# A decoder layer in float32: attention scores from 32-row tiles, a 9-column values product, residuals added on TensorE, and a new order of all engines

## The chip, the core and the metric

The kernel runs on one core of one Trainium2 chip. The metric is the device time of one execution in microseconds (us). Everything is float32.

## The reference, cut to what matters

The input `x` is 32 sequences (b) of 128 rows (s) by 128 features (d); `ctx` has the same shape. Three residual steps, each followed by a layer norm without gain:

```
# 1. self-attention, 16 heads of 8 features, keys and values through a rank-32 bottleneck
latent = (x@W_k + x@W_v) @ W_down_kv
k, v   = latent @ W_up_k, latent @ W_up_v ;  q = x @ W_q
scores = einsum('bhqd,bhkd->bhqk', q, k) / sqrt(128) * exp(-0.01*|i-j|)
x = layernorm(x + (softmax(scores) @ v) @ W_o)
# 2. second attention, over features: 8x8 weights in each head, from x and ctx
A = softmax_e(einsum('bhsd,bhse->bhde', x, ctx) / sqrt(128))
x = layernorm(x + ((ctx@Wv.T + bv) with A) @ Wo.T + bo)
# 3. experts: a norm with gain and offset, a router, the best 2 of 8 experts for each row
xf = layernorm(x, ln_g, ln_b) ;  logits = xf @ router ;  top 2, gates by softmax
each expert: layernorm(xf)*eg+eb -> clip/silu gated pair of 128x512 -> 512x128
x = layernorm(x + sum of the two gated experts)
```

## The kernel before, in words

The program has four blocks, one after the other, each with one instruction stream for every engine and semaphores between them.

The first block does attention, second attention and routing in one software pipeline. A loop runs over steps b = -1 to 38; in step b each engine does its part of several batches of different age: `on(b, lag)` is true when batch b - lag exists. Batch b has its input transposed and its queries and keys made in step b - 1, scores in step b, softmax and values product up to step b + 1, output projection and first norm in b + 2, the second attention in b + 3, its norm in b + 4, the router's norm in b + 5, router and choice in b + 6, and rank and scatter in b + 7. The order of an engine's instructions in a step is written out by hand.

Scores (`p_score`, L431): the keys of all heads stand in `kbd`, a block-diagonal image of 128 rows by 16 x 128 columns, so that one matmul of 512 columns gives four heads with the queries `qT` (128 rows) as weights. The image is made through DRAM: SP stores `kT` into a zeroed `key_image` (L250) and reads it back with four DMAs (L255). Two PSUM banks (`ps_s`) take the scores in turn. VectorE multiplies them by the decay into `sc` (L638, four a batch) and takes the row maximum of half the heads (L644, two a batch). GpSimd subtracts it (L332, `shift`, two a batch), and ScalarE exponentiates 1024 columns at a time (L551). TensorE transposes the 16 weight matrices (L411), ScalarE copies them out of PSUM (`a_pT`), and 16 matmuls sum into `acc` (`p_mix`, L422), each with one head of `vbd` as moving operand: 144 columns, 128 for the head's values in its own place with zeros around them and 16 for the row sums.

The first residual is an add on VectorE (L747) before statistics (L754), aggregation (L759), a power on GpSimd (L325, L327) and the norm `x1` (L764). After the second attention (masked gram matrix L701, maximum L725, exponential L600, `gA` L751, product L507, output L527) VectorE adds the residual (L655) and the bias (L668), takes statistics and norms into `xall` (L728). The router's norm is a statistics pair and norm again (L685, L711, L733), a gain and an offset on GpSimd (L373, L375) and a third norm `xhat` (L737). The router's choice ends in `both` on GpSimd (L379), two rank matmuls (L524, L525) and two indirect DMAs from GpSimd (L355) that put the rows into `expert_in`.

Before the loop SP issues, in this order: eleven loads of weights, the first input, all of `x` and of `ctx` (`xall`, `call`, four DMAs each of 512 KB, L224), three router parameters, the zeroing of the key images (L233). In the loop it loads each batch's `xin` and `cin` once more for the transposes (L240, L243). GpSimd issues the loads of the experts' parameters ahead of the loop (L313 to L320).

The second block works out the table of tiles from the counts (L788 on), the third runs the experts over 39 tiles of 256 rows, and the fourth gathers, adds, norms and stores.

Of the kernel before, what the change touches and what calls it, by code (L numbers as in the profile page):

```python
# [24 lines left out]
I32 = mybir.dt.int32  # L25
U32 = mybir.dt.uint32
# [10 lines left out]
def decoder_layer(nc, x, ctx_in, W_q, W_k, W_v, W_o, W_down, W_upk, W_upv, xWv, xbv, xWo, xbo,  # L37
# [9 lines left out]
    VW = D + H  # L47
# [7 lines left out]
    LOAD = 8  # L55
# [7 lines left out]

    GH = 32 // HD
    KIMG_H = HD * GH * S + S
    KIMG = GH * KIMG_H * (P // 32)
    kimg = nc.dram_tensor("key_image", [2, KIMG], F32)

    with ExitStack() as es:
# [6 lines left out]

        xall = sb("xall", [P, B, D])
        call = sb("call", [P, B, D])
        xf = sb("xf", [P, 2, D])
        gain_row = sb("gain_row", [P, D])  # L80
        offset_row = sb("offset_row", [P, D])
        rpad = sb("rpad", [P, P])
        xfT = sb("xfT", [P, S])
        top = sb("top", [P, B, E])
        thr = sb("thr", [P, MAXT]); tile_no = sb("tile_no", [P, TILES])
        idx = sb("idx", [P, 2, E], U32)
        iota_e = sb("iota_e", [P, E])
        oh = sb("oh", [P, 2, 2, E])
        both = sb("both", [P, E])
        cum = sb("cum", [P, E])  # L90
        rnk = sb("rnk", [P, 2, E])
        row_f = sb("row_f", [P, 2, 2])
        pos = sb("pos", [P, B, 2], U32)
        xhat = sb("xhat", [P, B, RW])
        fill = sb("fill", [P, 2, RW])
        earlier = sb("earlier", [P, P])
        ones = sb("ones", [P, P])
        iota_i = sb("iota_i", [P, B + 2 + 2 * E + MAXT + TILES], I32)
        st3 = sb("st3", [P, 6])
        st4 = sb("st4", [P, 6])  # L100
        mv34 = sb("mv34", [P, 2, 2]); rs34 = sb("rs34", [P, 2])
        xn = sb("xn", [P, D])
        params = sb("params", [P, E, PRM])
        bo_rows = sb("bo_rows", [P, E, D])
        ident = sb("ident", [P, P])
# [11 lines left out]
        eps_col = sb("eps_col", [P, 4])  # L117
        setup = sb("setup", [P, 8, D])
        xin = sb("xin", [P, 2, D])
        cin = sb("cin", [P, 2, D])  # L120
        x1 = sb("x1", [P, 2, D])
        xT = sb("xT", [P, 2, S])
        qT = sb("qT", [P, 2, S])
        kT = sb("kT", [P, 2, S])
        kbd = sb("kbd", [P, 2, H, S])
        vbd = sb("vbd", [P, 2, H, VW])
# [3 lines left out]
        rsum = sb("rsum", [P, 2, H])  # L130
        att = sb("att", [P, D])
        attT = sb("attT", [P, D])
        res1 = sb("res1", [P, D])
        st1 = sb("st1", [P, 6])
        mv1 = sb("mv1", [P, 2])
        rs1 = sb("rs1", [P, 1])
# [8 lines left out]
        res2 = sb("res2", [P, D])  # L145
        st2 = sb("st2", [P, 6])
        mv2 = sb("mv2", [P, 2])
        rs2 = sb("rs2", [P, 1])


        zrow = sb("zrow", [P, 4 * D])
        mv3, mv4 = mv34[:, 0, :], mv34[:, 1, :]
        rs3, rs4 = rs34[:, 0:1], rs34[:, 1:2]
# [4 lines left out]
        acc = ps_a[:, 0:VW]  # L158
        m0a, m0b = ps_m[:, 0, 0, :], ps_m[:, 0, 1, :]
        m1a, m1b = ps_m[:, 1, 0, :], ps_m[:, 1, 1, :]  # L160
        m2a, m2b = ps_m[:, 2, 0, :], ps_m[:, 2, 1, :]
        m0c, m2c, m2d = ps_m[:, 0, 2, :], ps_m[:, 2, 2, :], ps_m[:, 2, 3, 0:E]


        ld_w = sem("ld_w"); ld_x = sem("ld_x"); ld_c = sem("ld_c"); zeroed = sem("zeroed")
        x_in = [sem("x_in0"), sem("x_in1")]; c_in = [sem("c_in0"), sem("c_in1")]
        cst = sem("cst"); su_v = sem("su_v"); su_p = sem("su_p"); su_a = sem("su_a")
        x_trans = sem("x_trans"); xT_ready = sem("xT_ready")
        qk_done = sem("qk_done"); q_ready = sem("q_ready"); k_ready = sem("k_ready")
        v_done = sem("v_done"); v_ready = sem("v_ready")  # L170
        k_clear = sem("k_clear"); k_stored = [sem("k_stored0"), sem("k_stored1")]
        k_spread = [sem("k_spread0"), sem("k_spread1")]
        scored = sem("scored"); decayed = sem("decayed"); maxed = sem("maxed")
        shifted = sem("shifted"); exped = sem("exped")
        p_trans = sem("p_trans"); pT_ready = sem("pT_ready"); mixed = sem("mixed")
        sums_inv = sem("sums_inv"); att_ready = sem("att_ready"); att_trans = sem("att_trans")
        attT_ready = sem("attT_ready"); projected = sem("projected"); res1_ready = sem("res1_ready")
        stat1 = sem("stat1"); mean1 = sem("mean1"); rstd1 = sem("rstd1"); x1_ready = sem("x1_ready")
# [4 lines left out]
        res2a = sem("res2a"); res2_ready = sem("res2_ready"); stat2 = sem("stat2"); mean2 = sem("mean2"); rstd2 = sem("rstd2")  # L183
        x2_ready = sem("x2_ready")
        stat3 = sem("stat3"); mean3 = sem("mean3"); xn_ready = sem("xn_ready")
        gained = sem("gained"); xf_ready = sem("xf_ready")
        stat4 = sem("stat4"); mean4 = sem("mean4"); xhat_ready = sem("xhat_ready"); rstd34 = sem("rstd34")
        top_ready = sem("top_ready"); oh_ready = sem("oh_ready"); both_ready = sem("both_ready"); ranked = sem("ranked")
        cum_ready = sem("cum_ready"); rank_read = sem("rank_read"); row_ready = sem("row_ready"); pos_ready = sem("pos_ready")
        tagged = sem("tagged"); filled = sem("filled"); scattered = sem("scattered")  # L190
        f_trans = sem("f_trans"); fT_ready = sem("fT_ready"); routed = sem("routed"); logits_ready = sem("logits_ready")
        ld_p = sem("ld_p"); ld_e = sem("ld_e"); zero_row = sem("zero_row"); rcst = sem("rcst")
# [926 lines left out]
```

## Time and profile before

| | us |
|---|---|
| median of 3 runs | 889.16 (888.18 to 890.44) |
| profiled execution, its own time | 885.5 |
| its span, first to last instruction | 883.8 |
| mean granted TensorE clock, share of 2.4 GHz | 0.924 |

Of the span, the first block takes about the first 539 us, the table of tiles until 548, the experts until about 826 and the last block the rest. In the profile, "PE" is TensorE's matmuls and "PEld" its weight loads, DVE is VectorE, ACT ScalarE, POOL GpSimd, SP SyncE; an engine name with a q is its queue. A float32 matmul shows as two instructions. The end of a matmul is modelled; the starts are what can be compared.

### The profile page before, as it was taken

What the parts mean: (1) busy time and instruction counts of PE and PEld (TensorE: products, weight loads), DVE (VectorE), ACT (ScalarE), POOL (GpSimd) and SP (SyncE); (2) the same over time, 40 slices, a digit from 0 to 9 for tenths busy, and PEclk for the clock granted to TensorE, in tenths of its full rate; (3) what the DMA queues carried; (4) which work ended last, traced back from release to release, by engine and by line L of the source; (5) the groups of instructions that cost most, each with busy time, mean ns of one, the idle gap of its engine ahead of it and who ended that gap; (6) DMA issues with size and microseconds to landing.
All of it is one profiled execution on the core that took longest, in us unless ns stands there. A gap on an engine that the chain in (4) does not pass through costs nothing. (4 is left out here: it accounts for less than half of the span.)

```text
span 883.8 us, 14582 instructions
## 1 busy us (share of the span) xinstructions
PE 646.6 (73%) x3961; PEld 534.8 (61%) x3961; DVE 588.7 (67%) x1819; ACT 322.4 (36%) x756; POOL 458.8 (52%) x785
## 2 busy tenths in 40 slices
PE   1189988888889898989898530888888888885000
PEld 1057877777767676767677420777787878874000
DVE  2056886868687777778787433577777777774487
ACT  1034544444444443444444200444444444442000
POOL 9034547676666666666667671044343443434244
PEclk9999999999999999999999755899999999998555
DMA  8711111111111111111110000455555555551243
GB/s 196 146 43 40 43 43 31 52 35 48 37 45 38 45 37 46 46 37 55 28 49 16 16 24 20 152 167 165 151 171 159 171 163 157 176 167 52 79 120 92
DMA packets 86912, 74.18 MB, mean 84 GB/s; under 512 B 10896, under 2 KB 69840, under 8 KB 86832
## 3 DMA queue, kind: packets, MB, share of 16 engines
q1 hardware_dynamic: 76832, 60.14, 24.0%
q0 software_dynamic: 5392, 11.01, 4.0%
q10 hardware_dynamic: 4608, 2.10, 0.8%
q8 instruction: 33, 0.54, 0.3%
q14 instruction: 47, 0.39, 0.2%
HBM read 58.04 MB, written 15.17 MB: 83 GB/s over the span
## 5 line engine op out<-in xcount | busy, mean ns | idle before, releaser
L422 PE MATMUL ps_a<-vbd,pT 128*128 128x144 f32 x1024 | 149.8, 290 | 1.2 <-ACT pT L535 0.5
L422 PEld LDWEIGHTS ps_a<-vbd,pT 128*128 128x128 f32 x1024 | 134.8, 190 | 20.8 <-issue 15.5
L332 POOL TENSOR_TENSOR sc<-sc,rowmax 128x1024 f32<-128x1024 f32 x64 | 121.5, 1898 | 41.9 <-DVE rowmax L644 41.9
L431 PE MATMUL ps_s<-kbd,qT 128*128 128x512 f32 x256 | 132.6, 601 | 5.4 <-DMA kbd<-key_image 5.4
L638 DVE TENSOR_TENSOR sc<-ps_s,decay 128x512 f32<-128x512 f32 x128 | 87.4, 683 | 57.1 <-PE ps_s L431 56.4
L962 ACT ACTIVATE x2c<-ps_m,prt 128x256 f32<-128x256 f32 x117 | 55.5, 474 | 139.0 <-PE ps_m L927 139.0
L913 POOL DMA_INDIRECT expert_out<-yt,dest x78 | 82.8, 1062 | 34.3 <-issue 30.2
L938 PEld LDWEIGHTS ps_t<-wot,hid 128*128 128x128 f32 x624 | 92.6, 191 | 11.3 <-DVE hid L998 2.5
L535 ACT ACTIVATE pT<-ps_t 128x512 f32<-128x512 f32 x128 | 72.7, 596 | 70.0 <-PE ps_t L411 67.3
L925 PE MATMUL ps_m<-xg,w2t 128*128 128x256 f32 x234 | 74.0, 398 | 32.2 <-DVE hid L994 29.4
L938 PE MATMUL ps_t<-wot,hid 128*128 128x128 f32 x624 | 94.7, 275 | 1.9 <-DVE hid L998 1.9
L551 ACT ACTIVATE sc<-sc 128x1024 f32<-128x1024 f32 x64 | 68.0, 1062 | 48.4 <-POOL sc L332 48.4
L644 DVE TENSOR_REDUCE rowmax<-sc 128x8 f32<-128x1024 f32 x64 | 77.8, 1215 | 0.1
L355 POOL DMA_INDIRECT expert_in<-xhat,pos x64 | 65.0, 1016 | 19.6 <-POOL pos L348 9.9
L905 POOL COPY bot<-bo_rows 128x128 f32 x39 | 12.1, 310 | 114.6 <-DVE yt L1004 114.6
L411 PE MATMUL ps_t<-ident,sc 128*128 128x128 f32 x512 | 71.3, 273 | 0.0
L927 PE MATMUL ps_m<-xg,w1t 128*128 128x256 f32 x234 | 70.5, 383 | 0.0
L325 POOL TENSOR_TENSOR rs<-mv,eps_col 128x1 f32<-128x1 f32 x64 | 12.1, 189 | 111.6 <-DVE mv L759 80.1
L411 PEld LDWEIGHTS ps_t<-ident,sc 128*128 128x128 f32 x512 | 60.0, 141 | 16.3 <-issue 16.3
L994 DVE SCALAR_TENSOR_TENSOR hid<-ps_m,prt,sil 128x256 f32<-128x256 f32 x117 | 53.0, 481 | 23.9 <-ACT sil L968 23.8
L649 DVE RECIPROCAL rsum<-ps_a 128x16 f32<-128x16 f32 x32 | 8.2, 258 | 81.3 <-PE ps_a L422 81.3
L925 PEld LDWEIGHTS ps_m<-xg,w2t 128*128 128x128 f32 x234 | 36.0, 194 | 39.1 <-issue 32.6
(194 smaller groups left out, 1305.8 us busy)
## 6 DMA issues: line engine op xcount, KB each, us to landing
w2t<-in_L_ffn_W_dram SPq DMA_DIRECT2D x39, 256.0 KB, 2.7
w1t<-in_L_ffn_W_dram SPq DMA_DIRECT2D x39, 256.0 KB, 2.9
wot<-in_L_ffn_Wo_dram SPq DMA_DIRECT2D x39, 256.0 KB, 3.6
kbd<-key_image SPq DMA_DIRECT2D x128, 64.0 KB, 1.9
xst<-expert_in SPq DMA_DIRECT2D x39, 130.0 KB, 2.0
g<-expert_out SPq DMA_DIRECT2D x32, 128.0 KB, 2.1
xin<-in_x_dram SPq DMA_DIRECT2D x32, 64.0 KB, 2.0
xall<-in_x_dram SPq DMA_DIRECT2D x4, 512.0 KB, 6.7
```

Source lines behind the costliest of these rows:

```text
L332: pool.tensor_tensor(sc[:, slot], sc[:, slot], rowmax[:, slot, :].unsqueeze(2).to_broadcast([P, HALF, S]), ALU.subtract).then_inc(shifted, 1)
L411: mm = pe.transpose(ps_t[:, quarter % 2, j * S:(j + 1) * S], sc[:, 2 * par + quarter // 2, 4 * (quarter % 2) + j, :], ident[:, :])
L422: mm = pe.matmul(acc, pT[:, quarter, j * S:(j + 1) * S], vbd[:, par, h, :], start=(h == 0), stop=(h == H - 1))
L431: pe.matmul(ps_s[:, quarter % 2, :, :], qT[:, par, :], kbd[:, par, 4 * quarter:4 * quarter + 4, :], start=True, stop=True).then_inc(scored, 1)
L535: return act.activation(out, in_, ACT.Copy)
L551: act.activation(sc[:, slot], sc[:, slot], ACT.Exp).then_inc(exped, 1)
L638: dve.tensor_tensor(sc[:, slot, j:j + 4, :], ps_s[:, quarter % 2, :, :], decay[:, :].unsqueeze(1).to_broadcast([P, 4, S]), ALU.mult).then_ ...
L644: dve.tensor_reduce(rowmax[:, slot, :], sc[:, slot], AX.X, ALU.max).then_inc(maxed, 1)
L913: pool.indirect_dma_start(ys_dram[:, :], bass.IndirectOffsetOnAxis(ap=dest[:, n, a:a + 1], axis=0), yt[:, par, a, :], None).then_inc(y_out ...
L925: pe.matmul(ps_x2[c], w2t[:, par, P * c:P * c + P], xg[:, par, :], start=True, stop=True)
L927: pe.matmul(ps_x1[c], w1t[:, par, P * c:P * c + P], xg[:, par, :], start=True, stop=True).then_inc(up, 1)
L938: mm = pe.matmul(ps_y[par][:, a * P:(a + 1) * P], hid[:, par, c, a * P:(a + 1) * P], wot[:, par, c, :], start=(c == 0 and a == 0), stop=(c ...
```

## The change

All of it is in the first block.

- Scores: the key image has 128 rows by 4 x 128 columns (`kbd[P, 3, GH, S]`): rows 32g to 32g+31 hold heads 4g to 4g+3. One matmul has 32 rows of `qT` as weights and 32 rows of `kbd` as moving operand, again 512 columns and four heads. Two such matmuls, on neighbouring 32-row strips and into the two banks of `ps_s`, are issued behind each other with one semaphore. The image is stored and read back by one DMA each, without zeroing in SBUF, and `xT`, `qT`, `kT` and `kbd` have three buffers.
- Values product: `v9` holds 9 columns a head (8 values and a one for the sum); each matmul writes its own 9 columns of `acc`. ScalarE writes `v9`.
- Residuals: `ident` x `xall` is accumulated onto the projection, and `first` x `bo_row` and `ident` x `x1` onto the second output; statistics and norms read PSUM.
- The router's norm is worked out from the second norm's variance v: (v(1 + eps) + eps^2)^-0.5 scales `centred`, the centred rows times the gain; its own statistics are gone.
- Softmax: heads 0 to 7 are exponentiated by eight ScalarE instructions of 128 columns with the negated maximum as bias; heads 8 to 15 as before with GpSimd's shift.
- Loads: `x` and `ctx` come four batches at a time, from SP, every fourth step; the transposes read `xall` and `call`; the zeroing of the images is issued by ScalarE; the experts' parameters are loaded behind GpSimd's work of step 0.
- Each engine's loop runs over steps s = -2 to 39 with a new order, and the waits are rewritten for it.

```diff
 # SyncE
-                for dst, src, done in ((xall, x, ld_x), (call, ctx_in, ld_c)):
-                    for i in range(0, B, LOAD):
-                        sp.dma_start(dst[:, i:i + LOAD, :], ...)
+                sp.dma_start(xall[:, 1:4, :], x[1:4].rearrange("b s d -> s b d")).then_inc(ld_x, 16)
+                sp.dma_start(call[:, 0:4, :], ctx_in[0:4].rearrange("b s d -> s b d")).then_inc(ld_c, 16)
...
+                for b in range(B):
+                    spread_keys(b)      # wait k_ready; store kT; wait k_stored, scored of b - 3; read into kbd
+                    if b % 4 == 0 and b + 4 < B:
+                        n = b + 4
+                        sp.dma_start(xall[:, n:n + 4, :], x[n:n + 4].rearrange("b s d -> s b d")).then_inc(ld_x, 16)
+                        sp.dma_start(call[:, n:n + 4, :], ctx_in[n:n + 4].rearrange("b s d -> s b d")).then_inc(ld_c, 16)
 # GpSimd
+                for s in range(first_step, last_step + 1):
+                    if ever(s - 7): tag(s - 7)
+                    if ever(s - 4): rstd4_of(s - 4)
+                    if ever(s - 6): count(s - 6)
+                    if ever(s - 3): rstd2_of(s - 3)
+                    if ever(s - 3): router_rows(s - 3)
+                    if ever(s - 7): place(s - 7)
+                    if ever(s - 7): scatter(s - 7)
+                    if ever(s + 1): shift(s + 1)
+                    if ever(s - 5): choices(s - 5)
+                    if ever(s - 1): rstd1_of(s - 1)
+                    if s == 0:
+                        # params (10 DMAs) and bo_rows
 # TensorE
-                def p_score(b, quarter, par):
-                    ...
-                    pe.matmul(ps_s[:, quarter % 2, :, :], qT[:, par, :], kbd[:, par, 4 * quarter:4 * quarter + 4, :],
-                              start=True, stop=True).then_inc(scored, 1)
+                def score(b, pair):
+                    if pair == 0:
+                        pe.wait_ge(q_ready, b + 1)
+                        pe.wait_ge(k_spread[b % 2], 16 * (b // 2 + 1))
+                        before(pe, decayq[2], b)
+                        before(pe, decayq[3], b)
+                    else:
+                        pe.wait_ge(decayq[0], b + 1)
+                        pe.wait_ge(decayq[1], b + 1)
+                    for i in range(2):
+                        rows = slice(32 * (2 * pair + i), 32 * (2 * pair + i) + 32)
+                        mm = pe.matmul(ps_s[:, i, :, :], qT[rows, b % 3, :], kbd[rows, b % 3, :, :], start=True, stop=True)
+                    mm.then_inc(scored, 1)
-                        mm = pe.matmul(acc, pT[:, quarter, j * S:(j + 1) * S], vbd[:, par, h, :],
-                                       start=(h == 0), stop=(h == H - 1))
+                        mm = pe.matmul(acc[:, h, :], pT[:, i, j * S:(j + 1) * S], v9[:, b % 2, h, :], start=True, stop=True)
+                    pe.matmul(m0a, attT[:, :], wo[:, :], start=True, stop=False)
+                    pe.matmul(m0a, ident[:, :], xall[:, b, :], start=False, stop=True).then_inc(projected, 1)
...
+                    pe.matmul(m2a, oT[:, :], xwoT[:, :], start=True, stop=False)
+                    pe.matmul(m2a, first[:, :], bo_row[:, :], start=False, stop=False)
+                    pe.matmul(m2a, ident[:, :], x1[:, b % 2, :], start=False, stop=True).then_inc(x_out, 1)
+                def trans_f(s):
+                    b = s - 6
+                    upto(pe, x1_ready, s - 3)
+                    pe.wait_ge(xf_ready, b + 1)
+                    pe.transpose(m0c, xf[:, b % 2, :], ident[:, :]).then_inc(f_trans, 1)
...
+                for s in range(first_step, last_step + 1):
+                    if ever(s - 1): trans_p(s - 1, 1)
+                    if ever(s - 6): trans_f(s)
+                    if ever(s - 3): trans_c(s)
+                    if ever(s + 2): trans_x(s)
+                    if ever(s): score(s, 1)
+                    if ever(s + 2): queries(s)
+                    if ever(s + 2): keys(s)
+                    if ever(s - 1): trans_p(s - 1, 2)
+                    if ever(s - 3): vp(s)
+                    if ever(s - 2): trans_att(s)
+                    if ever(s - 1): trans_p(s - 1, 3)
+                    if ever(s - 3): gram_of(s)
+                    if ever(s - 6): logits(s)
+                    if ever(s - 1): mix(s - 1, 1)
+                    if ever(s - 1): mix(s - 1, 0)
+                    if ever(s - 2): project(s)
+                    if ever(s - 1): mix(s - 1, 3)
+                    if ever(s + 1): score(s + 1, 0)
+                    if ever(s): values(s)
+                    if ever(s - 3): second_out(s)
+                    if ever(s - 1): mix(s - 1, 2)
+                    if ever(s): trans_p(s, 0)
+                    if ever(s - 3): second_sum(s)
+                    if ever(s - 6): ranks(s)
 # ScalarE
+                def exp_heads(b):
+                    slot = 2 * (b % 2)
+                    act.wait_ge(maxed0, b + 1)
+                    for h in range(HALF):
+                        done = act.activation(sc[:, slot, h, :], sc[:, slot, h, :], ACT.Exp, bias=rowmax[:, slot, h:h + 1])
+                    done.then_inc(exped0, 1)
...
+                    # copy_p(s-2,3), gram_exp(s-4), exp_heads(s-1), copy_o(s-4), exp_half(s-1), copy_v(s-1),
+                    # copy_p(s-1,0), copy_x(s+2), copy_c(s-3), copy_f(s-6), copy_p(s-1,1), copy_k(s+2),
+                    # copy_q(s+2), copy_att(s-2), copy_vp(s-3), copy_p(s-1,2)
 # VectorE
+                def centred(b):
+                    dve.scalar_tensor_tensor(out=xc[:, b % 2, :], in0=m2a, scalar=mv2[:, 0:1], in1=gain_row[:, :],
+                                             op0=ALU.subtract, op1=ALU.mult).then_inc(xc_ready, 1)
...
+                for s in range(first_step, last_step + 1):
+                    # gram_max(s-3), best_index(s-6), row_max(s,1), gram_inv(s-3), second_weights(s-3) [gA],
+                    # one_hot(s-6), norm4(s-5) [xhat], stats1(s-2), aggr1(s-2), decayed_scores(s+1,1), stats4(s-4),
+                    # decayed_scores(s+1,0), norm1(s-2) [x1], aggr4(s-4), sums(s-1), heads(s-1), stats2(s-3),
+                    # aggr2(s-3), row_max(s+1,0), centred(s-3), norm2(s-3) [xall], decayed_scores(s+1,3),
+                    # own_rank(s-6), row_of(s-7), decayed_scores(s+1,2), masked_gram(s-2), best(s-5)
```

`upto(engine, semaphore, b)` waits until batch min(b, 31) has signalled. The calls of ScalarE's and VectorE's orders, and GpSimd's parameter loads, are written here as comments that list them.

## Rows read from the trace of the kernel before

**Rows 1.** Busy time by window: length, busy us and instructions per engine, clock, DMA.

```profile
300.00:400.00 100.00, 87.85 (x568) 70.36 (x567) 75.94 (x235) 44.01 (x112) 66.95 (x111) 1.00 0.15 42
500.00:520.00 20.00, 9.27 (x32) 7.11 (x32) 8.52 (x50) 2.14 (x8) 14.13 (x33) 0.50 0.06 20
580.00:700.00 120.00, 105.64 (x631) 94.56 (x632) 86.73 (x242) 54.28 (x111) 48.85 (x74) 1.00 0.53 163
```

**Rows 2.** Timeline, TensorE, the input transpose that opens a step: start, us.

```profile
96.83 0.27 PE L440 MATMUL ps_m<-ident,xin 128*128 128x128 f32 x1
108.52 0.27 PE L440 MATMUL ps_m<-ident,xin 128*128 128x128 f32 x1
...
310.39 0.27 PE L440 MATMUL ps_m<-ident,xin 128*128 128x128 f32 x1
324.81 0.27 PE L440 MATMUL ps_m<-ident,xin 128*128 128x128 f32 x1
```

**Rows 3.** Waits of TensorE, 200 to 400 us: us in total, times, longest.

```profile
PE ps_m L524 <- POOL both L379: 16.6, 14, 1.2
PE ps_m L507 <- DVE gA L751: 7.7, 14, 0.6
```

**Rows 4.** Timeline, TensorE, 300 to 315 us.

```profile
301.51 1.02 PE L431 MATMUL ps_s<-kbd,qT 128*128 128x512 f32 x2
302.36 1.14 PE L422 MATMUL ps_a<-vbd,pT 128*128 128x144 f32 x8
303.34 0.39 PE L496 MATMUL ps_m<-wo,attT 128*128 128x128 f32 x2
303.56 1.02 PE L431 MATMUL ps_s<-kbd,qT 128*128 128x512 f32 x2
...
308.67 0.36 PE L524 MATMUL ps_m<-both,earlier 128*128 128x8 f32 x2 [1.18 <-POOL both L379]
308.88 0.37 PE L525 MATMUL ps_m<-cum,ones 128*128 128x8 f32 x2
309.10 0.47 PE L527 MATMUL ps_m<-xwoT,oT 128*128 128x128 f32 x2
...
313.55 1.04 PE L411 MATMUL ps_t<-ident,sc 128*128 128x128 f32 x8
314.42 0.27 PE L482 MATMUL ps_m<-ident,att 128*128 128x128 f32 x1
```

**Rows 5.** Timeline, GpSimd and VectorE, 316 us.

```profile
316.40 1.90 POOL L332 TENSOR_TENSOR sc<-sc,rowmax 128x1024 f32<-128x1024 f32 x1
316.43 1.95 DVE L728 TENSOR_SCALAR xall<-res,mv,rs 128x128 f32<-128x128 f32 x1
```

**Rows 6.** Timeline, ScalarE, 201 us: an exponential with a bias and its successor.

```profile
201.18 0.40 ACT L600 ACTIVATE gex<-gm,gmax 128x128 f32<-128x128 f32 x1 [0.85 <-DVE gmax L725]
201.49 0.19 ACT L600 ACTIVATION_READ_ACCUMULATOR gex<-gm,gmax 128x1 f32 x1
```

**Rows 7.** Timeline, the start of the kernel, all engines.

```profile
11.29 14.87 SPq L224 DMA_DIRECT2D call<-in_ctx_dram  x4
11.63 0.79 PE L401 MATMUL ps_m<-setup 32*128 32x128 f32 x2 [0.36 <-ACT setup L535]
15.52 0.80 PE L453 MATMUL ps_m<-xT,wq 128*128 128x128 f32 x2 [1.65 <-ACT xT L535]
16.96 0.27 ACT L535 ACTIVATE kT<-ps_m 128x128 f32<-128x128 f32 x1
36.79 0.63 SPq L250 DMA_DIRECT2D key_image<-kT  x1
42.16 2.07 PE L431 MATMUL ps_s<-kbd,qT 128*128 128x512 f32 x2 [3.31 <-DMA kbd<-key_image]
```

**Rows 8.** Timeline, the last steps of the loop and the next block's first matmul.

```profile
500.78 0.57 PE L524 MATMUL ps_m<-both,earlier 128*128 128x8 f32 x2 [1.93 <-POOL both L379]
501.20 0.57 PE L525 MATMUL ps_m<-cum,ones 128*128 128x8 f32 x2
...
539.18 0.57 PE L788 MATMUL ps_a<-cum,ones 128*128 128x8 f32 x2 [11.76 <-PEq L209]
```

More of the change, by code:

```diff
@@ L201, in before, with ever, upto @@
                 eng.wait_ge(s, v)
-        def steps(step):
-            for b in range(-1, B + 7):
-                step(b, b % 2)
-        wsrc = [W_q, W_k, W_v, W_o, xWv, xWo]
+        def ever(b):
+            return 0 <= b < B
+        def upto(eng, s, b):
+            before(eng, s, min(b, B - 1) + 1)
+        first_step, last_step = -2, B + 7
         with nc.Block() as block:
@@ L530, in _, with trans_c @@
-                steps(step)
+                def trans_f(s):
[3 more added lines that the diff above has]
+                    pe.transpose(m0c, xf[:, b % 2, :], ident[:, :]).then_inc(f_trans, 1)
+                def trans_c(s):
+                    b = s - 3
+                    upto(pe, x1_ready, s - 3)
+                    pe.wait_ge(ld_c, 16 * (b // 4 + 1))
+                    pe.transpose(m0b, call[:, b, :], ident[:, :]).then_inc(c_trans, 1)
@@ new lines, in trans_x, with vp @@
+                def trans_x(s):
+                    b = s + 2
+                    upto(pe, x1_ready, s - 3)
+                    pe.wait_ge(ld_x, 16 * (1 if b == 0 else b // 4 + 2))
+                    pe.transpose(m0a, xall[:, b, :], ident[:, :]).then_inc(x_trans, 1)
+                def vp(s):
+                    b = s - 3
+                    upto(pe, xT_ready, s + 2)
+                    upto(pe, fT_ready, s - 6)
+                    pe.wait_ge(cT_ready, b + 1)
+                    pe.matmul(m0b, xwvT[:, :], cT[:, :], start=True, stop=True).then_inc(vp_done, 1)
@@ new lines, in trans_p @@
+                def trans_p(b, i):
+                    if i < 2:
+                        pe.wait_ge(exped0, b + 1)
+                        before(pe, pT_ready[i + 2], b)
+                    else:
+                        pe.wait_ge(exped1, b + 1)
+                        pe.wait_ge(pT_ready[i - 2], b + 1)
+                    for j in range(4):
+                        mm = pe.transpose(ps_t[:, i % 2, j * S:(j + 1) * S], sc[:, 2 * (b % 2) + i // 2, 4 * (i % 2) + j, :],
+                                          ident[:, :])
+                    mm.then_inc(p_trans[i], 1)
@@ L535, in copy @@
                     return act.activation(out, in_, ACT.Copy)
+                act.wait_ge(zeroed, 1)
+                for i in range(2):
+                    act.dma_start(kimg[i].rearrange("(p n) -> p n", p=P), zrow[:, :]).then_inc(k_clear, 16)
                 act.wait_ge(su_p, 1)
```

953 lines of the change are left out of this document (457 added, 496 removed).

## The prediction

> **What bounds the kernel now.** I read the windows first. From 60 to 480 us the kernel runs the attention and routing loop; from 580 to 800 it runs the expert stage, which this change does not touch. In the attention window TensorE is busy 88 of 100 us, VectorE 76, GpSimd 67, ScalarE 44 [rows 1]. Busy TensorE time is modelled, so I went to the timeline for the spacing of starts. One loop step, from one transpose of the inputs to the next, is 14.42 us (310.39 to 324.81); before the routing work joined, a step was 11.69 [rows 2]. So 26 of the 32 steps with scores (b = 6 to 31) cost 14.42.
>
> How much of a step does TensorE need? Its instructions follow each other at these pitches [rows 4]: a float32 matmul is two instructions; 512 columns cost 0.85 us the pair (301.51 to 302.36); eight instructions of 144 columns 0.98 (0.122 each); a 128-column float32 matmul 0.22; eight transposes 0.87 (0.109 each). The rows to look at are those with 8 columns: L524, L525 and L527 start 0.21 and 0.22 apart, so a two-instruction matmul costs 0.107 each whether it streams 8 or 128 columns. What is left then is the weight load. The step needs 4 x 0.85 = 3.4 for scores, 32 x 0.122 = 3.9 for the values product, 20 transposes 2.2, and 11 small matmuls 2.4: 11.9 us. The other 2.5 are stalls, of which 1.7 have a name: the rank matmul waits 1.2 us for GpSimd's `both`, the second attention 0.55 for VectorE's `gA` [rows 3]. Behind `gA` stands a stall of VectorE: the norm at L728 takes 1.95 us, from 0.03 after GpSimd's shift L332 starts to its end [rows 5]. TensorE is the bound, with 2.5 of its 14.4 us lost to the order of the engines' work.
>
> **The change part by part**, per step at the same pitches.
>
> Values product, 144 to 9 columns: the count stays 32 instructions and 32 weight loads. They fall from 0.122 to the floor of 0.107 [rows 4], 32 x 0.015 = 0.5 saved, giving 3.4. The columns fall sixteenfold and the time by an eighth. Less than nothing is excluded, since the 8-column rows show the floor directly; 0.5 is nearly certain.
>
> Scores from 32-row tiles in pairs: still 4 matmuls of 512 columns. Fewer rows alone buy nothing: L401 with 32 rows takes 0.79 where L453 with 128 rows takes 0.80, both at the low clock [rows 7]. A gain needs the two tiles of a pair to run beside each other. No row shows that. Bounds: each pair takes 0.85 (full overlap), or 1.71 (none). Each matmul is two instructions on the same rows that must follow each other, so the first tile's second half can lie beside the second tile's first half, and three half-matmuls remain: 3 x 0.427 = 1.28. I take that, in between. Against it stands the change of tile shape, twice per pair, four times a step. A 128-column transpose is recorded at 0.27 us and its neighbour starts 0.11 after [rows 2, 4], so 0.16 of it is still in the pipe; if the engine had to empty and then load weights uncovered (0.107), a change costs 0.16 + 0.1 = 0.26, four of them 1.0. Below that it can cost nothing. I take half, 0.5. Scores: 2 x 1.28 + 0.5 = 3.1, bounds 1.7 and 4.4, against 3.4 now.
>
> The skill bears on this place: the Trainium skill, TensorEngine Tiling, Key Properties, says that a change of tiling mode drains the engine while tiles of one mode run in parallel. By that rule the four changes cost their full 1.0 and the scores 3.6, so they would gain nothing; no row here shows a change of mode in a full stream.
>
> Residuals on TensorE: `ident` x `xall`, `first` x `bo_row`, `ident` x `x1` are three more small matmuls at 0.22: +0.66. The new step sum: values 3.4, transposes 2.2, small ones 2.4 + 0.66, scores 3.1 = 11.8 (8.7 without scores), against 11.9. The work of TensorE hardly falls; what can fall is the stall.
>
> VectorE, now 10.9 a step (76 per 100 us, [rows 1, 2]). Removed: two residual adds, the bias add, the third statistics pair, the norm `xn`, the copy into the diagonal (to ScalarE), some 1.2 together at 0.15 to 0.25 each; `norm2` now reads PSUM. Added: `centred`, 0.2. The stall behind the shift does not go: `norm4` is of the same form as L728, and it and `gA` now stand right behind `row_max(s,1)`, which releases the one shift that stays. So about 1.9 us is paid again in that place [rows 5]. Sum about 10. GpSimd: one of two shifts of 1.9 goes, the norm's `pow` chain gains one instruction: from 9.6 to about 8.5. ScalarE, 6.3 now: eight exponentials of 128 columns with a bias instead of one of 1024. The `gex` row of that shape starts its successor 0.31 later [rows 6]: 8 x 0.31 = 2.5 for about 1.1, with the value copy 0.2: 7.9. All stay below TensorE.
>
> The loops, followed through a step (TensorE time from its start). `score(s+1,0)` ends near 8.6; VectorE's two decays, `stats4` and `norm1` take 2.1; TensorE has 3.3 of other work before `trans_f` needs `x1_ready`: 1.2 slack. `gA`: the row maximum at 6.8, the shift until 8.9 at worst, `second_out` due near 9: no slack. `exped0` at about 8.5, due at 10.1 for `trans_p(s,0)`. `both` moves to a place two microseconds ahead of `ranks`. So the old 1.2 stall has cover, and the old 0.55 may stay. I put 0.35 of stalls: period 11.8 + 0.35 = 12.15. 26 steps x (14.42 - 12.15) = 59 us.
>
> The key path: SP stores and spreads in two DMAs for five, and no longer issues `xin` and `cin` each step; three buffers let it run a step ahead. It took 5.4 us from the store's issue to the first score (36.79 to 42.16, [rows 7]) against a period of 12: hidden. The 512 KB that SP issues every fourth step stand behind the spread and ahead of the next store, hidden by the same slack.
>
> The head: keys of batch 0 are ready at 17 (16.96, [rows 7]) and stored only at 36.79, because SP is held 15 us issuing the bulk loads of `call`, and rows and clears behind it. Those loads now come four batches at a time and the clear goes by ScalarE's queue at the start. First score at 17 + 5.4 = 22.4 for 42.2. The GpSimd fill of 1 MB may lie beside it: 20 saved, bounds 10 and 22. The ten parameter loads that GpSimd issues now stand behind its second shift; its next work is a step later. Early steps: two near 9.5 and four near 11.3 make 64 behind `score(0,0)`, against the 66 from 42.2 to 108.5 [rows 2, 7], and the first pair is at the low clock: nothing counted.
>
> The tail (steps 32 to 38, before L788 at 539.2, [rows 8]) is latency, with PE waiting for VectorE and GpSimd; the router rows no longer need a second `pow` round: 5 saved, bounds 0 and 12.
>
> **Sum.** 59 + 20 + 5 = 84 off the profiled execution's 885.5 (span 883.8 and 1.7 around it): 801.5. The median of the runs, 889.2, lies 3.7 above that execution, so 805 on its scale.
>
> **The rivals.**
> 1. Forecast: partial overlap, a step of 11.7 to 12.6. With 26 steps that is 793 to 817; with head and tail, 785 to 825. Chance 0.48.
> 2. Full overlap and free changes: scores 1.7, period 10.4 + 0.3 = 10.7, 38 us more: 767. For it: the tiles lie on separate rows and in separate PSUM banks. Against it: the two halves of one matmul, and loops with little slack. Chance 0.13.
> 3. The tiles bring nothing: pairs at 1.71 and full changes, 8.7 + 4.4 = 13.1, with stalls 13.45: 34 us more, 839. For it: no row shows overlap. Chance 0.2. The rule above would give 8.7 + 3.6 + 0.35 = 12.65, or 818, within rival 1.
> 4. A new wait: `gA` held by the shift makes `second_out` late by a microsecond, and copies, `second_sum` and the next statistics slide with it: 13.2 a step, 832. For it: the lock of [rows 5] now lies just ahead of `gA`. Against it: a slower TensorE gives slack back. Chance 0.12.
> 5. Slower: the clock. In the thin tail the granted clock is 0.50 with TensorE busy 9 of 20 us [rows 1], and L524 to L525 is 0.42 for 0.21 [rows 4, 8]. The new loop streams few columns through most of a step. If the chip takes that for idleness, weight loads double and a step is some 23. The gain of 84 is gone when the low clock holds for about 84 / (32 x 11.5) = 23% of the loop; at half of it, 985. Against it: the transposes and small matmuls now fill such stretches at clock 1.00 and it never fell there. Chance 0.06. The Trainium skill, TensorE: Matmul & The Clock Gate, Part 4, says transposes do not count as busy time for the clock; by it this rival would be likelier than I put it, and the steady clock of 1.00 with eight transposes in a row neither bears it out nor refutes it.
> 6. No change to speak of: 0.01.
>
> **How the numbers follow.** The range takes rivals 1, 3, 4 and, down to the edge, 2: 768 to 850 (839 plus a head that saves 10 less). Below lies half of rival 2, above rival 5 and a piece of 3, some 0.17. Of this kernel 0.3% is about what a measurement can tell. Faster 0.93, same 0.01, slower 0.06.
>
> **What would show it.** Right: the L422 counterpart at 0.107 pitch with 9 columns; starts of the input transposes 12.1 apart; a first score near 22; granted clock 1.00 to the tail; `norm4` or `gA` at 1.9 us. The pair's four starts tell the tiles: second tile starting with the first tile's second half means 1.28, at once with the first means 0.85, after it 1.71; a gap ahead of each pair is the change of shape. Wrong: a granted clock of 0.5 inside the loop, or a period above 13 with TensorE waiting for `gA`, `x1_ready` or ScalarE's copies.

## The result, and the profile after

The changed kernel takes 974.95 us (969.61 to 978.86, 4 runs) against 888.95 (888.18 to 890.44, 4 runs) of the kernel before: a ratio of 1.096, with a 95% interval of 1.089 to 1.103. It is 86 us slower where 84 us less had been forecast. Here and below a time is the median of all runs of a kernel, a ratio that of its fast runs alone, which leaves out the slowest run of e2, e8, e9 and e11. The profiled execution took 971.45 us, its span is 969.6, and its mean granted clock is 0.739.

The page of the changed kernel: busy time by engine, then the clock row of the picture in 40 slices.

```profile
span 969.6 us, 16064 instructions
...
PE 798.2 (82%) x4153; PEld 671.6 (69%) x4153; DVE 578.3 (60%) x1596; ACT 371.6 (38%) x1012; POOL 404.8 (42%) x785
...
PEclk9998755766656575565656665569999999999555
```

Read the last line first. In the loop most of the clock digits are 5 to 7, in tenths of full speed, where [rows 1] had 1.00. The windows of the changed kernel, in the columns of [rows 1]:

```profile
300.00:400.00 100.00, 100.00 (x523) 83.98 (x522) 63.56 (x166) 47.17 (x144) 48.81 (x96) 0.64 0.15 39
780.00:880.00 100.00, 88.10 (x526) 78.42 (x524) 72.20 (x202) 45.40 (x93) 40.71 (x62) 1.00 0.54 164
```

TensorE is now busy all of the time, no wait of TensorE is left in this window, and its clock is 0.64. Of the two levels, 1.2 and 2.4 GHz, it holds the lower for (1 - 0.64) / 0.5 = 72% of the time. VectorE and GpSimd are busy for less of it than in [rows 1]. The expert stage, second row, is as fast as before. Within one stretch of the loop the two levels lie beside each other:

```profile
300.00:306.00 6.00, 6.00 (x30) 5.73 (x29) 2.82 (x8) 1.99 (x4) 1.56 (x6) 0.50 0.00 0
306.00:313.00 7.00, 7.00 (x54) 5.91 (x55) 5.85 (x15) 5.87 (x20) 5.11 (x7) 0.99 0.11 31
313.00:326.00 13.00, 13.00 (x54) 10.16 (x51) 7.22 (x21) 3.64 (x11) 5.62 (x15) 0.50 0.07 22
```

Seven microseconds at full clock hold as many instructions (54) as the next thirteen at half. Which stretch comes before the fall is read in the timeline of TensorE:

```profile
306.06 1.13 PE L525 MATMUL ps_s<-kbd,qT 32*128 32x512 f32 x4
307.12 0.49 PE L454 MATMUL ps_m<-xT,wq 128*128 128x128 f32 x2
...
309.24 1.93 PE L546 MATMUL ps_a<-v,pT 128*128 128x9 f32 x16
311.03 0.47 PE L445 MATMUL ps_m<-wo,attT 128*128 128x128 f32 x2
311.33 0.39 PE L446 MATMUL ps_m<-xall,ident 128*128 128x128 f32 x2
311.56 0.96 PE L546 MATMUL ps_a<-v,pT 128*128 128x9 f32 x8
312.44 1.63 PE L525 MATMUL ps_s<-kbd,qT 32*128 32x512 f32 x4
...
315.02 1.72 PE L546 MATMUL ps_a<-v,pT 128*128 128x9 f32 x8
316.59 1.09 PE L536 MATMUL ps_t<-ident,sc 128*128 128x128 f32 x4
```

Two things are to be seen. The pair of tiles that starts at 306.06 has its successor 1.06 later: the two tiles run beside each other, since two 512-column matmuls in turn need 2 x 0.85 [rows 4]. And between 307.1 and 312.4 TensorE streams transposes, 128-column matmuls and 24 instructions of 9 columns. At 309.24 those have a pitch (start to start) of 0.11; in the pair behind them the clock falls, and at 315.02 eight of them take 1.57 until the next start, 0.196 each. The input transposes before steps 8 and 30 start at 114.63 and 496.60: 22 steps of 17.36 us, in the order of 15.2, 18.2 and 21.3 by how much low clock falls in each, where [rows 2] had 14.42.

The head is as the change wanted it. ScalarE, the DMA queue of SyncE and TensorE at the start of the changed kernel:

```profile
16.35 0.28 ACT L578 ACTIVATE kT<-ps_m 128x128 f32<-128x128 f32 x1 [1.31 <-PE ps_m L458]
16.71 0.63 SPq L223 DMA_DIRECT2D key_image<-kT  x1
18.80 0.64 SPq L227 DMA_DIRECT2D kbd<-key_image  x1
25.35 2.08 PE L525 MATMUL ps_s<-kbd,qT 32*128 32x512 f32 x4 [7.11 <-DMA kbd<-key_image]
```

The first scores start at 25.35 for 42.16 in [rows 7], 16.8 us earlier. From there to the end of the execution the changed kernel needs 946.1 us, the one before 843.3: 103 more, of which 26 x (17.36 - 14.42) = 76 are the steady steps, and the rest the early steps (37 to 87 us, 16.7 each for 11.7) and, by what is left over, about one slow step more at the loop's end.

### The profile page after: what moved, and what is told of

Read it like the earlier page. It is cut to its first block and busy times, and to the rows that moved or that the text cites. A ratio compares the mean times of both kernels' runs of the same rounds, so it can differ in the third digit from the quotient of the medians.

```text
span 969.6 us, 16064 instructions
## 1 busy us (share of the span) xinstructions
PE 798.2 (82%) x4153; PEld 671.6 (69%) x4153; DVE 578.3 (60%) x1596; ACT 371.6 (38%) x1012; POOL 404.8 (42%) x785
## 5 line engine op out<-in xcount | busy, mean ns | idle before, releaser
L546 PEld LDWEIGHTS ps_a<-v,pT 128*128 128x128 f32 x1024 | 166.8, 250 | 0.0
L546 PE MATMUL ps_a<-v,pT 128*128 128x9 f32 x1024 | 163.6, 293 | 0.0
L525 PE MATMUL ps_s<-kbd,qT 32*128 32x512 f32 x256 | 116.3, 1001 | 8.7 <-DMA kbd<-key_image 7.1
L536 PE MATMUL ps_t<-ident,sc 128*128 128x128 f32 x512 | 123.0, 390 | 0.0
L536 PEld LDWEIGHTS ps_t<-ident,sc 128*128 128x128 f32 x512 | 101.1, 224 | 3.2 <-issue 3.2
L321 POOL TENSOR_TENSOR sc<-sc,rowmax 128x1024 f32<-128x1024 f32 x32 | 60.5, 1891 | 93.7 <-DVE rowmax L722 93.7
L655 ACT ACTIVATE sc<-sc,rowmax 128x128 f32<-128x128 f32 x256 | 77.8, 388 | 0.0
L774 DVE TENSOR_SCALAR gA<-gex,gsum 128x128 f32<-128x128 f32 x32 | 57.5, 1797 | 1.1
L1038 PEld LDWEIGHTS ps_m<-xg,w1t 128*128 128x128 f32 x234 | 45.7, 195 | 6.6
```

Of the source, the lines that this page charges most:

```text
L525: mm = pe.matmul(ps_s[:, i, :, :], qT[rows, b % 3, :], kbd[rows, b % 3, :, :], start=True, stop=True)
L536: mm = pe.transpose(ps_t[:, i % 2, j * S:(j + 1) * S], sc[:, 2 * (b % 2) + i // 2, 4 * (i % 2) + j, :], ident[:, :])
L546: mm = pe.matmul(acc[:, h, :], pT[:, i, j * S:(j + 1) * S], v9[:, b % 2, h, :], start=True, stop=True)
L655: done = act.activation(sc[:, slot, h, :], sc[:, slot, h, :], ACT.Exp, bias=rowmax[:, slot, h:h + 1])
L1038: pe.matmul(ps_x1[c], w1t[:, par, P * c:P * c + P], xg[:, par, :], start=True, stop=True).then_inc(up, 1)
```

## The experiments

Twelve kernels were run. Three theories are set against each other. F says that the clock falls because TensorE streams too few columns; T says that the 32-row tiles bring it down; D says that dense work, without pauses, is throttled. Code in this section is cut to the lines that matter. The table collects the results. The step is the mean of 22 steps of the loop, the clock that of the window 200 to 400, and their product is about what TensorE's step would take at full clock, waits included where there are any.

| kernel | values, columns | scores | time, us | ratio (95%) | step, us | clock | product |
|---|---|---|---|---|---|---|---|
| before | 144 | 128 rows | 888 | 1 | 14.42 | 1.00 | 14.4 |
| e3 | 9 | 128 rows | 958.8 | 1.079 (1.076 to 1.082) | 17.11 | 0.80 | 13.7 |
| e12 | 72 | 128 rows | 930.0 | 1.049 (1.046 to 1.052) | 16.17 | 0.88 | 14.2 |
| e4 | 144 | tiles, unpaired | 914.6 | 1.031 (1.027 to 1.035) | 15.00 | 1.00 | 15.0 |
| changed | 9 | tiles | 975.0 | 1.096 (1.089 to 1.103) | 17.36 | 0.64 | 11.1 |
| e1 | 144 | tiles | 800.4 | 0.901 (0.899 to 0.904) | 11.71 | 1.00 | 11.7 |
| e2 | 32 | tiles | 843.1 | 0.946 (0.940 to 0.951) | 13.07 | 0.85 | 11.1 |
| e6 | 72 | tiles | 788.4 | 0.888 (0.886 to 0.889) | 11.37 | 0.99 | 11.3 |
| e10 | 72 | tiles | 784.1 | 0.883 (0.882 to 0.885) | 11.26 | 0.98 | 11.0 |
| e5 | 144 | 128 rows | 825.6 | 0.929 (0.928 to 0.931) | 12.62 | 1.00 | 12.6 |
| e11 | 9 | 128 rows | 862.5 | 0.965 (0.961 to 0.970) | 14.12 | 0.88 | 12.4 |
| e7 | 9 | tiles, other order | 988.5 | 1.116 (1.111 to 1.120) | 18.08 | 0.59 | 10.7 |
| e8 | 9 + 256-column fillers | tiles | 839.4 | 0.945 (0.944 to 0.947) | 12.92 | 1.00 | 12.9 |
| e9 | 9 + 8-column fillers | tiles | 999.8 | 1.124 (1.119 to 1.129) | 18.47 | 0.64 | 11.8 |

(The windows of e6 and e10 take in the end of their loops, where the clock falls as in every kernel. In 200 to 350 of e6 and 200 to 340 of e10 it is 1.00, so at full clock their steps are 11.3, not the product.)

**e1, the values product alone put back.** The changed kernel with the 144-column block-diagonal product of before:

```
-  mm = pe.matmul(acc[:, h, :], pT[...], v9[:, b % 2, h, :], start=True, stop=True)
+  mm = pe.matmul(ps_a[:, 0:D + H], pT[...], vbd[:, b % 2, h, :],
+                 start=(i == 1 and j == 0), stop=(i == 2 and j == 3))
```

> The changed kernel with only its values product undone: 144 columns against the block-diagonal tile again, all else (32-row tiles, order, residuals on TensorE) kept; the tile is cleared on VectorE after the decay is ready. Theory F (few columns let the clock fall): a long stretch of matmuls that stream 9 columns is taken for idleness; with 144 columns the granted clock is near 1.00 in the loop, a step costs 8.7 - 3.4 + 3.9 + 2 x 1.06 = 11.3 plus at most 0.6 of stalls, and the whole runs in 765 to 800. Rival T (the 32-row tiles are what brings the clock down, since three quarters of the rows stand idle in them): the clock stays at 0.6 to 0.75, the step above 17 and the time above 950. Rival D (dense work without pauses is throttled): as T.

800.35 us: sixteen times the columns in 32 instructions of a step, and 175 us less. Its loop window and its pair of tiles, in the window and timeline views:

```profile
200.00:400.00 200.00, 198.24 (x1493) 167.69 (x1492) 180.05 (x478) 130.97 (x397) 139.96 (x276) 1.00 0.15 43
```

```profile
306.42 1.13 PE L527 MATMUL ps_s<-kbd,qT 32*128 32x512 f32 x4
307.48 0.49 PE L465 MATMUL ps_m<-wvf,xT 128*128 128x128 f32 x2
307.82 0.46 PE L473 MATMUL ps_m<-vpT,gA 128*128 128x128 f32 x2
308.12 1.15 PE L548 MATMUL ps_a<-vbd,pT 128*128 128x144 f32 x8
```

The clock is 1.00, TensorE as busy as in the changed kernel: dense work as such is not throttled, and D falls. The pair still takes 1.06, so with 144-column values the tiles do the clock no harm. The gain of this run is that of the steady steps and the head: 26 x (14.42 - 11.71) = 70 and 17 are 87, measured 87.6.

**e2, the values product 32 columns wide.** The same per-head product with more columns: `VW = HD + 1` becomes `VW = 32`.

> The changed kernel with 32 columns in each values matmul instead of 9 (8 values, then ones), all else kept. The weight load stays the longer part, so at a given clock the pitch stays 0.107 and nothing is paid. Theory F: each instruction's streaming rises from 9 to 32 columns, a quarter of its pitch; the clock rises some way, 0.64 to 0.7 or 1.0, and the time lies between 780 and 960. Rivals T and D: clock and time as in the changed kernel, 970 within 1%.

843.09 us, clock 0.85: between 9 and 144 columns, as a dose should act.

**e3, the kernel before with the 9-column product alone.** 

```
-  VW = D + H
+  VW = HD + 1
-  mm = pe.matmul(acc, pT[...], vbd[:, par, h, :], start=(h == 0), stop=(h == H - 1))
+  mm = pe.matmul(acc[:, h, :], pT[...], vbd[:, par, h, :], start=True, stop=True)
```

> The kernel before with only the values product of 9 columns, each head in its own place of the accumulator. Theory F: the clock falls below 0.9 in the loop of 60 to 480 us, the step grows from 14.4 to 16 or more and the time is above 930. Rivals T and D: the clock stays 1.00, the step is 14.4 less at most 0.5, the time 873 to 890.

958.78 us. This one part alone makes the kernel before 71 us slower, at a clock of 0.80. All the rest of the change is absent. Its loop window:

```profile
200.00:400.00 200.00, 174.87 (x955) 140.82 (x955) 128.28 (x394) 73.60 (x186) 114.27 (x189) 0.80 0.13 36
```

**e4, the kernel before with 32-row tiles alone,** each still between other matmuls, not in pairs: `pe.matmul(ps_s[...], qT[rows, par, :], kbd[rows, par, :, :])` with `rows = slice(32 * quarter, 32 * quarter + 32)`.

> The kernel before with only the scores changed: 32 rows of queries and of compact keys in each of the four matmuls, not in pairs, one quarter after another as in the kernel before. Theory F: 512 columns still stream, so the clock stays 1.00; no overlap is possible, so scores still cost 3.4 a step, and what is added is the change of tile shape, eight times a step at 0 to 0.26: 885 to 950, by the pairs seen in the changed kernel (1.06 for 0.85 with two changes) near 0.1 each, so 905. Rival T: the clock falls below 0.9 and the time is above 930.

914.58 us, clock 1.00. A lone tile in the timeline:

```profile
306.07 1.12 PE L432 MATMUL ps_s<-kbd,qT 32*128 32x512 f32 x2
307.13 0.49 PE L454 MATMUL ps_m<-xT,wq 128*128 128x128 f32 x2
```

From its start to the next is 1.06 where the 128-row matmul had 0.85 [rows 4], and its successor needs 0.33 for the usual 0.22. So going into 32-row tiles and out costs 0.2 within and some 0.1 behind, for nothing in return when the tile is alone. That a lone tile takes the same 1.06 as a pair shows that in a pair the second tile costs nothing. Four a step are 1.3 us of TensorE's time, of which 0.58 shows in the step; the idle time of TensorE probably took the rest. T's claim of a falling clock is refuted here.

**e5, e1 with 128-row scores.** `pe.matmul(ps_s[:, i, :, :], qT[:, b % 3, :], kbd[:, b % 3, q4:q4 + 4, :])`, four read-back DMAs to the blocks, zeros between.

> The kernel of e1_values144 with the 32-row tiles undone too: block-diagonal keys of 128 rows by 2048 columns in SBUF, four read-back DMAs, the two matmuls of a pair still issued together. Clock 1.00 by both theories left. If the tiles overlap fully (1.06 a pair with two changes of shape, against 2 x 0.85), the step grows from 11.7 by 2 x 0.65 = 1.3 to 13.0 and the time by some 38 to 838. Rival (the gain of the changed kernel at full clock lies in the order alone, and the tiles bring nothing): within 0.5% of 800.

825.63 us. A pair takes 1.71 from its start to the next for e1's 1.06:

```profile
303.43 1.88 PE L531 MATMUL ps_s<-kbd,qT 128*128 128x512 f32 x4
305.14 0.38 PE L469 MATMUL ps_m<-wvf,xT 128*128 128x128 f32 x2
```

The step is 12.62 for 11.71: the tiles bring 0.9 a step and 25 us. More was expected, 1.3 a step, because 0.1 ahead of each pair and 0.1 behind it had not been counted.

**e6, two groups of 72 columns.** Eight heads share a group: `pe.matmul(ps_a[:, VB * half:VB * half + VB], pT[...], vbd[:, b % 2, h, :])` with `VB = 8 * VW`.

> The changed kernel with 72 columns in each values matmul: eight heads of 9 columns share a block-diagonal tile, in two groups, all else kept. 72 columns still stream in less than the weight load takes, so the pitch is 0.107 to 0.11 against 0.126 with 144. Theory F: half of each pitch streams; if that is enough for the clock (1.00), the step is 11.1 and the time 780 to 788; if it is not (clock 0.9 to 0.97), 790 to 820. Rival (the clock wants the full 144): a clock near that of 32 columns, 0.85, and 835 or more.

788.43 us, just above the 780 to 788 expected, the steady step 11.33 at clock 1.00. Half the columns of e1 keep the clock here, and the narrower product takes some 0.37 us off e1's step.

**e7, the 9-column product spread over more of the step:** `mix(1)` ahead of the Gram matrix, `mix(0)` behind the projection, `score(s + 1, 0)` ahead of `mix(3)`.

> The changed kernel, 9 columns kept, with TensorE's own order altered in one place: the values matmuls are spread (mix 1, gram, logits, project, mix 0, score(s+1,0), mix 3) where they stood in one run (mix 1, mix 0, project, mix 3, score). The same instructions and columns. If it is the long thin stretch that lets the clock fall, the clock rises from 0.64 to above 0.8 and the time falls below 900. If the mean over the step decides, clock and time stay, 955 to 985.

988.48 us, clock 0.59. This order rescues nothing, so the one run of 9-column products is not what decides. The stretch between the two score pairs, which has no wide matmul, is only one group of eight shorter than in the changed kernel (200.16 to 208.58 here, 286.80 to 296.93 there, both at the low clock), so its length is not tested by this run.

**e8 and e9, fillers.** To the changed kernel four matmuls a step are added whose results nobody reads, once with 256 columns and once, as control, with 8:

```
+  if j == 2:
+      pe.matmul(ps_a[:, 256:512], ident[:, :], setup[:, 0:2, :]..., start=True, stop=True)   # e8
+      pe.matmul(ps_a[:, 256:264], ident[:, :], setup[:, 0, 0:8], start=True, stop=True)      # e9
```

> The changed kernel, 9 columns kept, with one matmul of 256 columns added in the middle of each group of four values matmuls; its result goes to unused columns of the accumulator's bank and nobody reads it. It adds four times 2 x 0.213 = 1.7 us of work to a step at the full clock. Theory F (columns streamed hold the clock): granted clock above 0.95, a step of 13.0 to 13.4, and the time 830 to 870: more work, and 100 us faster than the changed kernel. Rival (it is the form of the values product, nine columns written once against an accumulated sum, and not the streaming): the clock stays at 0.6 to 0.7 and the time rises above 1000.

> The control of e8_filler256: the same added matmuls with 8 columns, so the same weight loads and instructions and no streaming to speak of; 0.86 us a step at the full clock. Theory F: the clock stays at 0.55 to 0.7 and the time rises to 990 to 1040. If an interruption of the run of values matmuls or the instruction count were what holds the clock, it would rise as in e8_filler256.

More work makes the kernel 136 us faster: 839.39 us. The same number of instructions with 8 columns makes it 25 slower: 999.75. The loop windows of e8 and e9:

```profile
200.00:400.00 200.00, 200.00 (x1490) 170.37 (x1489) 168.93 (x436) 121.41 (x371) 125.51 (x250) 1.00 0.17 44
```

```profile
200.00:400.00 200.00, 200.00 (x1046) 169.23 (x1044) 116.41 (x304) 85.59 (x262) 87.24 (x172) 0.64 0.11 30
```

The number behind the length is TensorE's busy time, 200 of 200 in both. In e8 it gets 1490 instructions done, in e9 1046. The values product itself is the same as in the changed kernel, so neither its many groups nor its target in PSUM brings the clock down, and e9 rules out the count of instructions: what differs between e8 and e9 is the columns streamed.

**e10, e6 with the second attention's weights scaled on ScalarE.** `act.activation(gA[:, :], gex[:, :], ACT.Identity, scale=gsum[:, 0:1])` takes the place of VectorE's multiplication.

> The kernel of e6_values72 with gA (second attention weights) scaled on ScalarE in place of VectorE, which waits there until GpSimd's shift has ended. If that stall is what TensorE's few remaining waits for gA come from, they go and the time is 781 to 786; if TensorE's own work is the whole bound, 788 within 0.4%. norm4 then stands behind the shift and takes its 1.9 us.

784.14 us, the fastest of all: 11.7% below the kernel before. The group of `gA` in e6, and in e10, 200 to 400 us:

```profile
L787 DVE TENSOR_SCALAR gA<-gex,gsum 128x128 f32<-128x128 f32 x18 | 36.2, 2010 | 0.6
```

```profile
L683 ACT ACTIVATE gA<-gex,gsum 128x128 f32<-128x128 f32 x18 | 7.0, 388 | 0.5 <-DVE gsum L788 0.5
```

2010 ns on VectorE beside GpSimd's shift, 388 on ScalarE. This agrees with the Trainium skill, SBUF — State Buffer, "SBUF: two separate sides", by which some VectorE instructions and GpSimd's take a shared pair of ports as a lock for a whole instruction, while ScalarE never waits for it. On the path the stall was worth little, 4.3 us.

**e11, the changed kernel with 128-row scores.** The edit of e5 with 9-column values; it completes the square of the two parts.

> The changed kernel with its 9-column values product, but the scores again from 128-row blocks of keys (two matmuls of 512 columns one after the other, a pair 1.71 us at full clock for the tiles' 1.06). Question: do the overlapping tiles take part in the fall of the clock? If what counts is how much of a step TensorE streams columns (F, all of the step), the pair that streams 0.65 us longer, twice a step, lifts the loop's clock from 0.64 to 0.72 to 0.85, the step from 17.6 to 15 to 16.5, and the kernel ends at 900 to 950 us: slower tiles make it faster. If only the thin values product and what stands beside it matter (F, the stretch), the clock stays at 0.60 to 0.66 and the longer pairs are paid on top: 985 to 1020 us. The 144-column pair of the same two kernels went the ordinary way: 25 us slower with 128-row scores.

862.53 us, at a clock of 0.88. Scores that take 0.65 us longer a pair at full clock make the kernel 112 us faster. This is 37 us below the 900 to 950 that F had given for it: the direction was right, the size too small. Its windows of two microseconds:

```profile
308.00:310.00 2.00, 2.00 (x21) 2.00 (x19) 1.39 (x7) 1.68 (x6) 0.97 (x2) 1.00 0.13 33
310.00:312.00 2.00, 2.00 (x20) 2.00 (x19) 1.96 (x6) 2.00 (x8) 1.67 (x3) 1.00 0.54 82
312.00:314.00 2.00, 2.00 (x8) 1.26 (x8) 2.00 (x4) 1.07 (x4) 1.73 (x2) 0.64 0.38 115
314.00:316.00 2.00, 2.00 (x4) 0.69 (x3) 0.32 (x2) 0.00 (x0) 0.90 (x3) 0.51 0.00 0
316.00:318.00 2.00, 2.00 (x20) 2.00 (x19) 1.82 (x6) 1.37 (x4) 0.00 (x0) 1.00 0.00 0
```

The clock falls behind the thin stretch as before, but comes back at the end of the score pair in which it fell: the low level lasts less than 4 us for the 13 above. The pair in the timeline:

```profile
312.49 3.66 PE L530 MATMUL ps_s<-kbd,qT 128*128 128x512 f32 x4
315.98 0.39 PE L468 MATMUL ps_m<-wvf,xT 128*128 128x128 f32 x2
```

In some steps the clock does not fall at all (12.2 us each, three in a row from 254.93 to 291.60).

**e12, the kernel before with 72 columns.** The edit of e6 alone.

> The kernel before with one edit: the values product in two groups of 72 columns (eight heads each) instead of one of 144. F: 32 matmuls of 72 columns keep the clock at 1.00 in this kernel too, and they save at most 32 x 0.016 = 0.5 us a step of 14.42; the step is set in part by waits, so 0.1 to 0.5 a step or 3 to 13 us: 875 to 886, ratio 0.985 to 0.997. Rival: this kernel has idle TensorE time that the changed one lacks, and the clock falls below 1.00: over 895.

929.95 us, 1.049, at a clock of 0.88. The expectation of 875 to 886 was wrong: 72 columns keep the clock in the order of e6 and lose it in that of the kernel before. Its windows, and its longest waits of TensorE in 200 to 400:

```profile
312.00:314.00 2.00, 1.77 (x14) 1.63 (x14) 2.00 (x5) 0.77 (x2) 0.93 (x3) 1.00 0.04 11
314.00:316.00 2.00, 0.83 (x4) 0.86 (x5) 0.34 (x2) 0.00 (x0) 1.92 (x5) 0.64 0.00 0
316.00:318.00 2.00, 2.00 (x11) 2.00 (x12) 0.00 (x0) 0.00 (x0) 1.72 (x3) 0.50 0.00 0
```

```profile
PE ps_m L526 <- POOL both L380: 17.0, 13, 1.3
PE ps_m L509 <- DVE gA L753: 8.7, 12, 0.7
```

TensorE ends its 72-column products near 313.9 and then waits 1.31 for `both`, until 315.17; the fall lies in that stall. The kernel before has the same stalls [rows 3] and kept 1.00 with 144 columns, so here it took both the stalls and the narrower product. That stalls are also what sets this kernel apart from e6 was not tested by itself. 72 columns are not safe in every order.

## Why the prediction was wrong

**The step that failed** is the chance of rival 5, and behind it the reason against it: "the transposes and small matmuls now fill such stretches at clock 1.00 and it never fell there". That the clock held in the kernel before was taken as a property of the small matmuls. It depended on the wide matmuls that stood between them. e3 shows it: take the columns out of the values product alone and the clock falls to 0.80. The square shows how the two parts act together, in us:

| | 144 columns | 9 columns | |
|---|---|---|---|
| 128-row scores, one after the other | 825.6 | 862.5 | +37 |
| tiles in pairs | 800.4 | 975.0 | +175 |
| | -25 | +112 | |

Each part is cheap or good while the other is absent. Both take streaming out of the step: the values product by narrowing, the pairs by letting two streams pass at once. Together they cost 138 us more than their sum. That both the product's width and the pair's length act through the clock is shown by the clock of the four, 1.00, 0.88, 1.00 and 0.64, and by the fillers, which change neither and restore it.

The values product was called "nearly certain" to save 0.5 a step. At full clock it does save about that: e11's undisturbed steps are 12.22 for e5's 12.62, 0.40, and the pitch of 0.11 at 309.24 is the floor of [rows 4]. The sum priced every part at clock 1.00, and that condition failed. At full clock it was close, in part by luck: e1 gained 87.6 and e6 99.5 for the forecast 84, with a step shorter than forecast and a head and tail that gave less (below).

**The price of rival 5** was sound. It gave 985 for the low clock on half of the loop's work. Clock 0.64 over time is 1 / 0.64 - 1 = 0.56 of the work; by the same formula 801.5 + 0.56 x 32 x 11.5 = 1008, and less the 26 x (12.15 - 11.1) = 27 us by which the full-clock step was overrated (below), 981; measured 971.45. What was wrong was 0.06 for a rival with a price of 180 us, with a range that ended at 850.

The Trainium skill, TensorE: Matmul & The Clock Gate, Part 4, cited against the forecast, says that transposes do not count as busy time for the clock in the same way. The trace is in line with it, since in the changed kernel 20 transposes a step in an unbroken stream do not hold the clock; but 128-column and 9-column matmuls stand among them, and no run separates the transposes.

**The tiles.** Forecast was a pair of 1.28 and 0.25 for the changes of shape at it, 1.53. The trace of e1 answers the question of the four starts: 306.42, 306.42, 306.95 and 306.96. Measured: full overlap, 0.85, with 0.2 within the pair (e1: 1.06) and by e5 another 0.2 around it (1.71 - 1.25 = 0.46 a pair, twice a step, is the 0.9 found), so 1.25 and scores of 2.5 a step for 3.1. "Three half-matmuls remain" was wrong: both instructions of one tile run beside both of the other. The rule of the Trainium skill, TensorEngine Tiling (Array Packing), Key Properties, that a change of tiling mode drains the engine, agrees with the 0.3 of e4. Pairing pays for it: 825.6 to 800.4. Rival 2 was right on the overlap and wrong on the free changes.

**The step at full clock,** 12.15 forecast, is 11.71 in e1, 11.33 in e6, 11.25 in e10 and by the product 11.1 in the changed kernel. So the forecast was 0.8 to 1.1 too high for the narrow product: 0.6 by the scores, and the 0.35 put down for stalls, which are absent (no wait of TensorE in the steady steps of the changed kernel). The residuals' three matmuls cost 0.22 to 0.23 each, as forecast (L446 to its successor, 311.33 to 311.56).

**The lock** moved, as forecast, to the stretch behind the one shift that stays, and it hit `gA`, not `norm4`. In the columns of the page's costliest groups, changed kernel:

```profile
L655 ACT ACTIVATE sc<-sc,rowmax 128x128 f32<-128x128 f32 x256 | 77.8, 388 | 0.0
...
L774 DVE TENSOR_SCALAR gA<-gex,gsum 128x128 f32<-128x128 f32 x32 | 57.5, 1797 | 1.1
```

Rival 4's microsecond a step is not there: e10, which takes the stall away, gains 0.08 us a step over e6. The eight exponentials come from the first row: 77.8 / 32 = 2.43 a step for the forecast 2.5.

**Head and tail.** The head gave 16.8 of the forecast 20: from the store's issue (16.71) to the first score it took 8.6 us for the forecast 5.4, 6.5 of it from the read-back's issue (18.80). Tail and early steps together gave nothing of the forecast 5: in e1, 774.2 us from the first score to the end against 843.3 are 69 less, of which the steady steps are 70.

## What to carry to other kernels

Before columns are taken out of a TensorE stream that is bound by weight loads, price the clock as a term of its own: here the gain at constant clock was 0.4 us a step, the loss 5.7 (17.36 against 11.7). Read the granted clock of each stretch beside the busy share. A TensorE that is 100% busy in the profile can stand at half clock (313 to 326 above). When two parts of a change both shorten the time in which TensorE streams, try them alone and together; the best version kept the tiles, the new order and a wider product, of 72 columns (784 us for 975).

## What the runs showed of the hardware

- An unbroken stream of TensorE instructions doesn't hold the clock: 200 of 200 us busy at 0.64 with 9 columns in the values product, at 1.00 with 144.
- Added work can pay: four 256-column matmuls a step whose results are unread took 136 us off, four of 8 columns added 25.
- The values product in e1 and in the kernel before multiplies mostly zeros and holds the clock: zeros among what is streamed do not keep the clock from holding at 1.00.
- Two float32 matmuls in separate 32-row tiles overlap entirely (1.06 for both in e1, 1.06 for a lone one in e4, 0.85 for a 128-row one); a lone excursion into the tiles costs some 0.3.
- Open: how much streaming in which stretch keeps the clock. 72 columns were enough in one order and not in another (e6, e12), and in e11 the clock is back at the end of the slowed 128-row pair, which took 3.49 us (312.49 to 315.98), while in the changed kernel it stays low behind the tiles' 2.58 (312.44 to 315.02). These runs bound it for this kernel only.
